# Expert outputs scattered into token order tile by tile, and loaded densely in the last stage

## The chip, the cores and the metric

The kernel runs on one core of a Trainium2 chip. A core has five engines that work side by side, each on its own instruction stream: PE (TensorE, matmuls and transposes), DVE (VectorE), ACT (ScalarE), POOL (GpSimd) and SP (SyncE, which mostly issues DMAs). They meet through semaphores. Sixteen DMA engines move data between device memory and the on-chip memory SBUF; matmul results land in PSUM. The metric is the device time of one launch in microseconds (us).

## What is computed

One layer of an audio tower over 16 x 256 tokens of width 256, in float32: a token projection with a GELU, attention with 16 heads, and a mixture of experts with two of eight experts per token plus a gated shared expert. The part that matters here:

```python
logits = xf @ router_w
probs = jax.nn.softmax(logits, axis=-1)
topw, topi = jax.lax.top_k(probs, 2)
combine = jnp.zeros((n, 8)).at[jnp.arange(n)[:, None], topi].add(topw)
h = silu(jnp.einsum('nd,edf->nef', xf, w1))
ye = jnp.einsum('nef,efd->ned', h, w2)
routed = jnp.einsum('ne,ned->nd', combine, ye)
gu = xf @ shared_gate_up
shared = silu(gu[:, :256]) * gu[:, 256:] @ shared_down
return routed + sigmoid(xf @ shared_gate_w) * shared
```

The residual stream is added, and token 0 of each of the 16 sequences is left out of the output, so a sequence gives 255 rows.

## The kernel before

Tokens are worked on in 8 groups of 512 (4 tiles of 128 rows). There are three blocks with a barrier at the end of each: `token_phase`, `attention_phase` and `expert_phase`. Float32 products are made of three passes over high and low parts (`three`, L65 to L67), so each operand is split into a `_hi` part (a copy) and a `_lo` part (a subtraction).

`attention_phase` is one software pipeline: 8 groups of 16 units, where the router of group g-1 runs between the units of group g. For each row the router finds two slots (`slot_now`) in a table `x_slots` in device memory in which every expert has its own region. In units 12 to 15 POOL scatters the normalised rows `z2` into it with 8 indirect DMAs (L1102), two per unit. The router of the last group has no attention beside it: it runs alone after group 7. `tables` on DVE then makes the list of row tiles per expert, and SP and ACT fill the rest of each expert's last tile (`fill_up`). POOL waits for its scatters, and the block's barrier follows (L343).

`expert_phase` starts with a loop over 72 tiles of 128 rows. SP loads tile n+6 into `xg` (L1227) and stores the result of tile n from `yg` into `y_slots` in slot order (L1232). PE transposes, multiplies by the expert's two matrices and transposes between them; ACT and DVE make the high and low parts; DVE copies the result to `yg` (L1494). PE sets the order. Experts 0 and 1 are loaded and split by ACT and DVE, experts 2 to 7 and the shared expert are loaded on POOL's queue (L1210, L1211) and split by POOL (L1600, L1604); six weight splits and a larger one of the shared expert.

The last stage goes over the 8 groups. PE computes the shared expert (`shared_hidden`, `transpose_z`, `shared_rows`); ACT, DVE take turns behind it. Once all tiles are stored, POOL fetches each token's two expert rows with `gather`: per tile a copy of two slot numbers to `place_now` (L1620) and two indirect DMAs (L1624) into `back`. DVE adds them, weighted (`add_back`, L1554), then the gated shared rows (`add_shared`, L1565). SP stores a group with two DMAs:

```python
sp.dma_start(out[bass.ds(2 * g, 2), 0:P - 1, :].rearrange("b p d -> p b d"),
             rows[1:P, :, 0, :]).then_inc(s_out, 16)          # L1237: 127 partitions
sp.dma_start(out[bass.ds(2 * g, 2), P - 1:N - 1, :].rearrange("b p d -> p b d"),
             rows[:, :, 1, :]).then_inc(s_out, 16)            # L1239: 128 partitions
```

`z`, the normalised input of the shared expert, is loaded by ACT two groups ahead, 512 KB at a time (L1458).

## Time and profile before

| | us |
|---|---|
| median of 3 runs (lowest, highest) | 1255.91 (1255.13, 1256.11) |
| span of the profiled execution | 1250.2 |
| busy: PE | 1076.8 (86%) |
| busy: DVE | 834.0 (67%) |
| busy: ACT | 676.0 (54%) |
| busy: POOL | 342.7 (27%) |
| DMA, all sixteen engines, moved | 64.31 MB |

The page gives no time of the profiled execution other than its span; the runs' median is 5.7 us longer, and that difference is start and end outside the span. Times in the rows are microseconds from the span's start. "Idle before" in brackets names what ended the wait. A POOL row DMA_INDIRECT is the time in which POOL makes the descriptors, not the transfer. SPq, ACTq and PEq rows are the sequencer's own: the time that a DMA's issue holds the queue. Indirect transfers stand in queue q0, SP's in q1, ACT's in q10.

### The profile page before, as it was taken

To read this page: it belongs to the slowest core of one execution; us is meant where nothing else is said; L and a number is where in the kernel's file an instruction comes from. 1 tells how busy PE (TensorE), PEld (TensorE's weight loads), DVE (VectorE), ACT (ScalarE), POOL (GpSimd) and SP (SyncE) were. 2 spreads that over 40 slices of the span, in tenths; PEclk is the share of its full clock that TensorE was granted. 3 is DMA by queue.
4 is the path that set the end of the run, shared out by engine and by line. 5 is a ranking of instruction groups with operands and counts; after the bars stand their busy time and mean duration, and the time that the engine had idled before them with its cause. 6 is when DMAs were issued, how large, how long until landed. Compare 5 with 4: busy or idle time off the path is not lost. (4 is left out here: it accounts for less than half of the span.)

```text
span 1250.2 us, 26008 instructions
## 1 busy us (share of the span) xinstructions
PE 1076.8 (86%) x8010; PEld 884.1 (71%) x8011; DVE 834.0 (67%) x2247; ACT 676.0 (54%) x2116; POOL 342.7 (27%) x405
## 2 busy tenths in 40 slices
PE   7989999999999999999999999999732999987770
PEld 6766787777767778677777877877622899976660
DVE  3757758876885885888578588588544555655661
ACT  4557647755773774776476477477412455532210
POOL 0021212242132124224213322411314800026660
PEclk9989999999999999999999999999965999998885
DMA  7100000000000000000000000000005544434531
GB/s 239 48 5 1 1 2 18 1 35 18 0 17 18 17 0 34 17 0 25 26 0 9 25 17 0 34 18 1 35 37 190 174 135 134 148 115 130 164 111 55
DMA packets 46177, 64.31 MB, mean 51 GB/s; under 512 B 6232, under 2 KB 38744, under 8 KB 46104
## 3 DMA queue, kind: packets, MB, share of 16 engines
q1 hardware_dynamic: 35832, 37.51, 9.2%
q0 software_dynamic: 7328, 20.72, 4.9%
q10 hardware_dynamic: 2944, 5.24, 1.3%
q8 instruction: 29, 0.48, 0.2%
q14 instruction: 44, 0.36, 0.1%
HBM read 36.07 MB, written 27.38 MB: 51 GB/s over the span
## 5 line engine op out<-in xcount | busy, mean ns | idle before, releaser
L702 ACT ACTIVATE prob<-s_ps,nmax 128x255 f32<-128x255 f32 x512 | 239.6, 481 | 275.1 <-DVE nmax L815 273.4
L1084 POOL TENSOR_SCALAR prob<-prob,rinv 128x255 f32<-128x255 f32 x128 | 126.2, 986 | 599.7 <-DVE rinv L834 599.7
L560 PE MATMUL o_ps<-probT,v 128*64 128x256 f32 x1024 | 140.4, 393 | 45.2 <-ACT probT L727 43.4
L815 DVE TENSOR_REDUCE nmax<-s_ps 128x2 f32<-128x510 f32 x256 | 165.0, 675 | 19.0 <-PE s_ps L532 9.4
L560 PEld LDWEIGHTS o_ps<-probT,v 128*64 128x64 f32 x1024 | 70.5, 137 | 108.0 <-ACT v L723 52.2
L547 PE MATMUL pT_ps<-ident,prob 128*128 128x128 f32 x1024 | 134.0, 274 | 0.1
L547 PEld LDWEIGHTS pT_ps<-ident,prob 128*128 128x128 f32 x1024 | 115.6, 141 | 2.5 <-DVE prob L837 1.5
L837 DVE TENSOR_SCALAR prob<-prob,rinv 128x255 f32<-128x255 f32 x256 | 106.9, 460 | 4.5
L702 ACT ACTIVATION_READ_ACCUMULATOR prob<-s_ps,nmax 128x1 f32 x512 | 109.0, 213 | 0.0
L843 DVE COPY probT<-pT_ps 128x512 f32<-128x512 f32 x128 | 87.0, 680 | 8.5 <-PE pT_ps L547 7.9
L532 PE MATMUL s_ps<-k_hi,q_lo 64*128 64x256 f32 x512 | 85.7, 331 | 0.7 <-DVE k_lo L822 0.7
L65 PE MATMUL v_ps<-wv_hi,zT_lo 128*128 128x256 f32 x256 | 85.2, 333 | 0.8 <-ACT v L723 0.8
L832 DVE TENSOR_SCALAR rsum_eps<-rsum 128x4 f32<-128x4 f32 x128 | 21.6, 169 | 92.7 <-ACT prob L702 91.0
L727 ACT ACTIVATE probT<-pT_ps 128x512 f32<-128x512 f32 x128 | 77.3, 604 | 0.8 <-PE pT_ps L547 0.8
L532 PEld LDWEIGHTS s_ps<-k_hi,q_lo 64*128 64x128 f32 x512 | 48.2, 185 | 39.5 <-issue 19.9
L1102 POOL DMA_INDIRECT expert_in_rows<-z,slot_now x64 | 64.2, 1004 | 36.2 <-DVE slot_now L916 20.4
L1624 POOL DMA_INDIRECT back<-expert_out_rows,place_now x64 | 63.8, 998 | 35.7 <-POOL place_now L1620 21.9
L65 PE MATMUL proj_ps<-wo_hi,oT_lo 128*128 128x256 f32 x256 | 73.2, 286 | 0.0
L67 PE MATMUL v_ps<-wv_hi,zT_hi 128*128 128x256 f32 x256 | 72.5, 283 | 0.0
L66 PE MATMUL v_ps<-wv_lo,zT_hi 128*128 128x256 f32 x256 | 72.4, 283 | 0.0
L532 PE MATMUL s_ps<-k_lo,q_hi 64*128 64x256 f32 x512 | 72.4, 279 | 0.0
L66 PE MATMUL proj_ps<-wo_lo,oT_hi 128*128 128x256 f32 x256 | 72.4, 283 | 0.0
(250 smaller groups left out, 2983.2 us busy)
## 6 DMA issues: line engine op xcount, KB each, us to landing
xg<-expert_in_rows SPq DMA_DIRECT2D x72, 128.0 KB, 2.0
expert_out_rows<-yg SPq DMA_DIRECT2D x72, 128.0 KB, 1.9
xin<-in_x_dram SPq DMA_DIRECT2D x8, 512.0 KB, 4.9
z_rows<-z SPq DMA_DIRECT2D x8, 512.0 KB, 2.6
z<-z_rows ACTq DMA_DIRECT2D x7, 512.0 KB
out_dram<-resid SPq DMA_DIRECT2D x8, 256.0 KB
out_dram<-resid SPq DMA_DIRECT2D x8, 254.0 KB
raw_up<-in_L_ffn_w_dram POOLq DMA_DIRECT2D x6, 256.0 KB, 4.6
```

The source lines that it names most:

```text
L65: pe.matmul(out, wl, xh, start=start, stop=False, skip_group_check=True)
L66: pe.matmul(out, wh, xl, start=False, stop=False, skip_group_check=True)
L67: return pe.matmul(out, wh, xh, start=False, stop=stop, skip_group_check=True)
L532: m = pe.matmul(s_ps[h][:, qt * N:(qt + 1) * N], a[part, rows], k[part, keys], start=n == 0, stop=n == 2)
L547: m = pe.transpose(pT_ps[h][:, o:o + P], prob[u_par(i)][:, h, qt, kt * P:(kt + 1) * P], ident[:])
L560: m = pe.matmul(o_ps[h * DH:(h + 1) * DH, 0:N], vt[:, 2 * b + kt, col:col + DH], probT[u_par(i)][:, h, kt, :], start=kt == 0, stop=kt == 1)
L702: m = act.activation(prob[u_par(i)][:, h, qt, 1:N], s_ps[h][:, qt * N + 1:(qt + 1) * N], ACT.Exp, bias=nmax[u_par(i)][:, n:n + 1], accum_o ...
L727: act.activation(probT[u_par(i)][:, 0, :, :], pT_ps[0][:].rearrange("p (k q) -> p k q", k=2), ACT.Copy).then_inc(s_pA, 1)
L815: dve.tensor_reduce(nmax[u_par(i)][:, 2 * h:2 * h + 2], s_ps[h][:].rearrange("p (q k) -> p q k", q=2)[:, :, 1:N], AX_X, ALU.max, negate=Tr ...
L837: m = dve.tensor_scalar(prob[k][:, 0, qt, 1:N], prob[k][:, 0, qt, 1:N], rinv[k][:, qt:qt + 1], None, ALU.mult)
L843: dve.tensor_copy(probT[u_par(i)][:, 1, :, :], pT_ps[1][:].rearrange("p (k q) -> p k q", k=2)).then_inc(s_pB, 1)
L1084: pool.tensor_scalar(prob[k][:, 1, 0, 1:N], prob[k][:, 1, 0, 1:N], rinv[k][:, 2:3], None, ALU.mult).then_inc(s_nB, 1)
```

## The change

Each row now carries where its result belongs. `x_slots` gets 8 more columns per row (`XW` = 264); before each scatter POOL writes the row's place in token order, 2 x token + choice, into column 256 of `z2`, and the second scatter of a tile waits for the first one to land, since the mark is overwritten. The spare rows get places behind the real ones, so that SP and ACT store two DMAs per padded region instead of one, and 8 spare tiles are stored at the start of attention. In the expert loop DVE copies the places from `xg` to `y_at`, and POOL scatters each finished tile straight into token order; SP only loads. The experts' weights from the third on are loaded on SP's queue, and POOL splits them between its scatters. The last stage loads 1 MB per group densely into one of two buffers, which lie where `raw_up` was. ACT scales the first choice's rows, POOL adds them and also makes the low part of the hidden activations, DVE adds the second choice's. Semaphores of the first two blocks are merged without a change in what waits for what.

```diff
+XW = D + 8
+SPARE = TILES - TOP * ROWS // P
@@ attention_phase, SP @@
+            for n in range(SPARE):
+                pad(sp, x_slots[E * CAP + n * P:E * CAP + (n + 1) * P, :], E + n)
...
-                sp.wait_ge(s_scat, 16 * GT * TOP * (r + 1))
+                for t in range(GT):
+                    sp.wait_ge(s_scat[t], 16 * TOP * r + 16 * TOP)
@@ attention_phase, POOL, units 12 to 15 @@
+                    for t in (2 * half, 2 * half + 1):
+                        if n > 0:
+                            pool.wait_ge(s_scat[t], 16 * TOP * r + 16)
+                        pool.sem_inc(s_pgo, 1)
+                        pool.tensor_scalar(z2[:, t, D:D + 1], dest[:, t:t + 1], float(n), None,
+                                           ALU.add).then_inc(s_marked, 1)
+                        pool.wait_ge(s_marked, TOP * GT * r + GT * n + t + 1)
+                        pool.sem_inc(s_pgo, 1)
                         pool.indirect_dma_start(
-                            x_slots, bass.IndirectOffsetOnAxis(ap=slot_now[:, n // TOP, n % TOP:n % TOP + 1], axis=0),
-                            z2[:, n // TOP, :], None).then_inc(s_scat, 16)
+                            x_slots, bass.IndirectOffsetOnAxis(ap=slot_now[:, t, n:n + 1], axis=0),
+                            z2[:, t, :], None).then_inc(s_scat[t], 16)
@@ expert_phase, SP @@
-                sp.dma_start(y_slots[bass.ds(P * n, P), :], yg[k % BUFS][:]).then_inc(s_st[k % BUFS], 16)
+            def load_back(g, k):
+                sp.dma_start(back[k].rearrange("p t k d -> p (t k d)"),
+                             y_rows[bass.ds(TOP * GR * g, TOP * GR), :].rearrange("(p s) d -> p (s d)", s=TOP * GT)
+                             ).then_inc(s_back[k], 16)
...
-            for k in range(BUFS):
-                sp.sem_inc(s_st[k], FREE_D)
             for k in range(BUFS):
                 load(0, k, True)
+            for e in range(BY_POOL, E):
+                load_expert(sp, e)
+            sp.dma_start(raw_gu[:], gate_up.rearrange("(c p) f -> p c f", p=P)).then_inc(s_raw_gu, 16)
...
-            with sp.Fori(0, GROUPS - 2) as g:
-                store_group(g)
+            for k in range(UNROLL):
+                sp.wait_ge(s_st[k], 16 * TURNS)
+            for k in range(2):
+                load_back(k, k)
+            with sp.Fori(0, GROUPS // 2 - 1) as h:
+                for k in range(2):
+                    sp.wait_ge(s_used, 2 * GT * h + GT * k + GT)
+                    load_back(2 * h + k + 2, k)
+                    store_group(2 * h + k)
@@ expert_phase, ACT, before the next group's SiLUs @@
+            def scale_first(g, k, at):
+                act.activation(share_first[:], shares[:, bass.ds(GT * g, GT), 0:1], ACT.Copy).then_inc(s_share1, 1)
+                act.wait_ge(s_back[k], at)
+                act.wait_ge(s_share1, g + 1)
+                for t in range(GT):
+                    act.activation(back[k][:, t, 0, :], back[k][:, t, 0, :], ACT.Copy,
+                                   scale=share_first[:, t, :]).then_inc(s_scaled, 1)
@@ expert_phase, DVE, in x_lo @@
+                if not isinstance(r, int) or r > 0:
+                    dve.wait_ge(s_st[k], 16 * r)
+                dve.tensor_copy(y_at[k][:], xg[k % BUFS][:, D:D + 1]).then_inc(s_at, 1)
@@ expert_phase, POOL @@
+                pool.wait_ge(s_at, n + 1)
+                pool.wait_ge(s_yc, n + 1)
                 pool.sem_inc(s_pgo, 1)
-                for k in range(TOP):
-                    pool.indirect_dma_start(back[:, t, k, :], None, y_slots,
-                                            bass.IndirectOffsetOnAxis(ap=place_now[:, t, k:k + 1], axis=0)
-                                            ).then_inc(s_back[t], 16)
+                pool.indirect_dma_start(y_rows, bass.IndirectOffsetOnAxis(ap=y_at[k][:, 0:1], axis=0), yg[k][:], None
+                                        ).then_inc(s_st[k], 16)
+            between = {(0, 5): 4, (0, 11): 5, (1, 5): 6, (1, 11): 7}
...
+            def add_first(g, k):
+                for t in range(GT):
+                    rows = resid[:, GT * g + t, :]
+                    pool.wait_ge(s_scaled, GT * g + t + 1)
+                    pool.tensor_tensor(rows, rows, back[k][:, t, 0, :], ALU.add).then_inc(s_first, 1)
```

The order in which the engines get their instructions shows three places. First POOL, the router of the last group up to the block's end; before:

```order
L1092 TENSOR_SCALAR var_eps<-mean_var 128x4 [waits row_mean_var]
L1094 TENSOR_TENSOR rstd<-var_eps,half_neg 128x4 [waits row_var_eps]
L1102 DMA expert_in_rows<-z,slot_now 33920x256 [waits slots_ready]
L1102 DMA expert_in_rows<-z,slot_now 33920x256 x7
L343 UNCONDITIONAL_BRANCH [waits rows_scattered]
```

and of the change:

```order
L1125 TENSOR_SCALAR dest<-dest 128x4
L1133 TENSOR_SCALAR z<-dest 128x1 [waits slots_ready,dest_ready]
L1137 DMA expert_in_rows<-z,slot_now 34816x264 [waits rows_marked]
L1133 TENSOR_SCALAR z<-dest 128x1
L1137 DMA expert_in_rows<-z,slot_now 34816x264 [waits rows_marked]
...
L1133 TENSOR_SCALAR z<-dest 128x1 [waits rows0_scattered]
L1137 DMA expert_in_rows<-z,slot_now 34816x264 [waits rows_marked]
...
L349 UNCONDITIONAL_BRANCH [waits rows2_scattered,rows3_scattered,rows1_scattered,rows0_scattered]
```

Eight scatters in a row have become eight pairs of a mark (`z<-dest`) and a scatter that waits for it. Next POOL in the expert block, from the weights on (`back` is fetched by gathers before; `up_space` is the memory of `raw_up`); before:

```order
L1600 CAST up_hi<-raw_up 128x2x256 [waits expert_split,expert2_in]
...
L1604 TENSOR_TENSOR sd_lo<-raw_sd,sd_hi 128x512
L1620 COPY place_now<-places 128x2 [waits all_yg_stored,places_ready]
L1624 DMA back<-expert_out_rows,place_now 128x256 [waits place_now_ready]
L1624 DMA back<-expert_out_rows,place_now 128x256
```

and of the change:

```order
L1633 TENSOR_TENSOR dn_lo<-raw_down,dn_hi 128x2x256
L1652 DMA expert_out_rows<-yg,y_at 10240x256 [waits y_at_ready,yg_ready] x6
L1629 CAST up_hi<-up_space 128x2x256 [waits expert4_in]
L1629 CAST dn_hi<-raw_down 128x2x256
L1633 TENSOR_TENSOR up_lo<-up_space,up_hi 128x2x256 [waits expert_hi_by_pool]
L1633 TENSOR_TENSOR dn_lo<-raw_down,dn_hi 128x2x256
L1652 DMA expert_out_rows<-yg,y_at 10240x256 [waits y_at_ready,yg_ready] x6
```

POOL, which had nothing between its last split and the end of the loop, now has 72 scatters there, six between two splits. Last SP in the last stage; before:

```order
L1260 UNCONDITIONAL_BRANCH [waits yg4_stored,yg3_stored,yg5_stored,yg2_stored,yg0_stored,yg1_stored]
...
L1237 ISA [waits rows_complete]
L1237 REGISTER_ALU
L1237 DMA out_dram<-resid 127x2x256
L1239 ISA
L1239 DMA out_dram<-resid 128x2x256
```

and of the change:

```order
L1267 ISA [waits back_used]
L1267 DMA up_space<-expert_out_rows 128x2048
L1272 ISA
L1274 ISA [waits rows_complete]
L1274 REGISTER_ALU
L1274 DMA out_dram<-resid 127x2x256
L1276 ISA
L1276 DMA out_dram<-resid 128x2x256
```

The load of the group after next stands on SP's queue ahead of each pair of stores.

## Rows read from the trace of the kernel before

**Rows 1.** Windows: busy us (instructions) per engine, PE clock, DMA share, GB/s.
```profile
core 0: us, PE busy (x) PEld busy (x) DVE busy (x) ACT busy (x) POOL busy (x), PEclk, DMA share, GB/s
1040.00:1060.00 20.00, 19.90 (x169) 19.54 (x168) 12.47 (x33) 10.93 (x33) 0.00 (x0) 1.00 0.42 127
...
1180.00:1200.00 20.00, 15.63 (x99) 13.75 (x97) 12.64 (x28) 6.38 (x11) 12.93 (x19) 1.00 0.44 135
...
1225.00:1230.00 5.00, 0.00 (x0) 0.00 (x0) 1.71 (x5) 0.00 (x0) 0.00 (x0) 0.50 0.07 24
```

**Rows 2.** Timeline of POOL, last stage: start, us, engine, line, instruction, [idle before].
```profile
1125.70 0.19 POOL L1620 COPY place_now<-places 128x2 uint32 x1
1126.70 0.98 POOL L1624 DMA_INDIRECT back<-expert_out_rows,place_now  x1 [0.81 <-POOL place_now L1620]
1127.98 0.97 POOL L1624 DMA_INDIRECT back<-expert_out_rows,place_now  x1 [0.30 <-issue]
```

**Rows 3.** Timeline of SP's queue, last stage: first store, longest hold, last hold.
```profile
1133.18 0.33 SPq L1237 DMA_DIRECT2D out_dram<-resid  x1
...
1177.15 14.53 SPq L1239 DMA_DIRECT2D out_dram<-resid  x1
...
1232.92 10.76 SPq L1239 DMA_DIRECT2D out_dram<-resid  x1
```

**Rows 4.** DMA view of 1225 to 1250.2 us, in 40 slices.
```profile
GB/s 24 24 24 23 24 24 24 24 24 24 24 23 244 195 24 24 24 24 24 23 24 24 24 24 24 23 24 24 24 24 189 247 28 23 24 24 24 24 20 0
```

**Rows 5.** DMA view of 1134.3 to 1250.2 us: packets, MB, share of 16 engines.
```profile
q0 software_dynamic: 2497, 6.82, 20.4%
q1 hardware_dynamic: 4214, 4.18, 10.7%
q10 hardware_dynamic: 576, 2.10, 5.3%
```

**Rows 6.** Timeline of POOL in a unit of the attention loop.
```profile
783.95 1.09 POOL L1102 DMA_INDIRECT expert_in_rows<-z,slot_now  x1 [0.18 <-issue]
...
786.33 0.74 POOL L1078 TENSOR_TENSOR resid<-resid,bo_row 128x256 f32 x1
788.33 0.99 POOL L1084 TENSOR_SCALAR prob<-prob,rinv 128x255 f32<-128x255 f32 x1 [1.26 <-DVE rinv L834]
```

**Rows 7.** Timeline at the hand-over: first and last of eight scatters, the next block.
```profile
934.73 1.09 POOL L1102 DMA_INDIRECT expert_in_rows<-z,slot_now  x1 [20.44 <-DVE slot_now L916]
...
943.79 0.97 POOL L1102 DMA_INDIRECT expert_in_rows<-z,slot_now  x1 [0.30 <-issue]
...
951.96 1.23 DVE L1507 TENSOR_SCALAR passed<-slots,skips 128x64 f32<-128x64 f32 x7 [8.48 <-PEq L343]
```

**Rows 8.** Chain of waits at SP's start in the expert block: start, us.
```profile
952.28 0.28 SPq L1226
```

**Rows 9.** First tiles: POOL's splits, DVE's split of expert 1, SP, PE, window.
```profile
969.22 0.66 POOL L1600 CAST up_hi<-raw_up 128x512 fp32r<-128x512 f32 x1
...
973.00 0.60 POOL L1600 CAST up_hi<-raw_up 128x512 fp32r<-128x512 f32 x1
...
963.46 0.68 DVE L1475 TENSOR_TENSOR dn_lo<-raw_down,dn_hi 128x512 fp32r<-128x512 f32 x1
...
969.26 0.34 SPq L1227 DMA_DIRECT2D xg<-expert_in_rows  x1
...
975.23 0.44 PE L1277 MATMUL xgT_ps<-ident,xg 128*128 128x128 f32 x2 [2.09 <-DMA xg<-expert_in_rows]
...
965.00:969.00 4.00, 3.86 (x32) 3.83 (x33) 1.94 (x5) 2.17 (x7) 4.00 (x7) 1.00 0.99 345
```

**Rows 10.** Timeline of ACT and DVE ahead of the first store.
```profile
1118.72 1.15 ACT L1451 ACTIVATE h_hi<-h_full 128x512 fp32r<-128x512 f32 x2
...
1125.94 1.09 ACT L1437 ACTIVATE z3T_hi<-xgT_ps 128x512 fp32r<-128x512 f32 x2 [1.20 <-PE xgT_ps L1338]
...
1131.23 1.66 DVE L1565 SCALAR_TENSOR_TENSOR resid<-y_ps,gate_now,resid 128x256 f32 x4 [0.32 <-issue]
```

**Rows 11.** Instructions on tile `back`: duration ns min/median/max, first and last start.
```profile
L1624 POOL DMA_INDIRECT back<-expert_out_rows,place_now x64: 952/980/1502, 1113.5 to 1218.8; - x64
```

More of the change, by code:

```diff
@@ L195, in _ @@
         def _(pe):
-            pe.wait_ge(s_ident, 1)
+            pe.wait_ge(s_const, IDENT_SET)
             pe.wait_ge(s_ro, 16)
@@ L1158, in sem @@
             return ctx.enter_context(nc.semaphore(name))
-        raw_up, raw_down = sb("raw_up", [P, DC, E, F]), sb("raw_down", [P, FC, E, D])
+        up_space = sb("up_space", [P, DC * E * F])
+        raw_up = up_space[:].rearrange("p (c e f) -> p c e f", c=DC, e=E)
+        back = [up_space[:, k * GT * TOP * D:(k + 1) * GT * TOP * D].rearrange("p (t k d) -> p t k d", t=GT, k=TOP)
+                for k in range(2)]
+        raw_down = sb("raw_down", [P, FC, E, D])
         raw_gu, raw_sd = sb("raw_gu", [P, DC, 2 * F]), sb("raw_sd", [P, FC, D])
@@ L1464, in _ @@
             group(0, True, True, True)
-            with act.Fori(1, GROUPS - 2) as g:
-                group(g, False, True, True)
+            with act.Fori(0, GROUPS // 2 - 2) as h:
+                for k in range(2):
+                    scale_first(2 * h + k, k, 16 * h + 16)
+                    group(2 * h + k + 1, False, True, True)
+            scale_first(GROUPS - 4, 0, 16 * (GROUPS // 2 - 1))
+            group(GROUPS - 3, False, True, True)
+            scale_first(GROUPS - 3, 1, 16 * (GROUPS // 2 - 1))
             group(GROUPS - 2, False, True, False)
+            scale_first(GROUPS - 2, 0, 16 * (GROUPS // 2))
             group(GROUPS - 1, False, False, False)
+            scale_first(GROUPS - 1, 1, 16 * (GROUPS // 2))
         @block.vector
@@ L1567, in add_shared, with group @@
                                                  op1=ALU.add).then_inc(s_all, 1)
-            def group(g, first, last):
+            def group(g, k, first, last):
                 product(g, 0)
-                if not first:
-                    add_back(g - 1, 1)
                 product(g, 1)
@@ L1628, in _, with split_shared @@
-            pool.wait_ge(s_places, 1)
-            pool.wait_ge(s_stored, 1)
-            for t in range(GT):
-                gather(0, t, True)
-            with pool.Fori(1, GROUPS) as g:
-                for t in range(GT):
-                    gather(g, t, False)
+                split(e - BY_POOL, [(raw_up[:, :, e, :], up_hi[:, :, e, :], up_lo[:, :, e, :]),
+                                    (raw_down[:, :, e, :], dn_hi[:, :, e, :], dn_lo[:, :, e, :])], s_w)
+            def split_shared():
+                pool.wait_ge(s_raw_gu, 32)
+                split(E - BY_POOL, [(raw_gu[:], gu_hi[:], gu_lo[:]), (raw_sd[:], sd_hi[:], sd_lo[:])], s_gu_w)
@@ new lines, in _, with shared_lo @@
+            for r in range(2):
+                for k in range(UNROLL):
+                    scatter(r, k)
+                    if (r, k) in between:
+                        split_expert(between[r, k])
+            split_shared()
+            with pool.Fori(2, TURNS) as r:
+                for k in range(UNROLL):
+                    scatter(r, k)
+            def shared_lo(g):
+                for c in range(FC):
+                    pool.wait_ge(s_hhi, FC * g + c + 1)
+                    pool.tensor_tensor(h_lo[:, c, :], h_full[:, c, :], f32(h_hi[:, c, :]), ALU.subtract).then_inc(s_hlo, 1)
@@ new lines, in add_first @@
+            def add_first(g, k):
+                for t in range(GT):
+                    rows = resid[:, GT * g + t, :]
+                    pool.wait_ge(s_scaled, GT * g + t + 1)
+                    pool.tensor_tensor(rows, rows, back[k][:, t, 0, :], ALU.add).then_inc(s_first, 1)
+            shared_lo(0)
+            with pool.Fori(0, GROUPS // 2 - 1) as h:
+                for k in range(2):
+                    add_first(2 * h + k, k)
+                    shared_lo(2 * h + k + 1)
+            add_first(GROUPS - 2, 0)
```

242 lines of the change are left out of this document (111 added, 131 removed).

## The prediction

> **What bounds the kernel now.** I read the page's busy shares first, then the windows stage by stage, then each engine's timeline at the places that the diff touches, then the DMA view of the end. PE (TensorE) is busy for most of the span, so the question is what the change does where PE is not the limit. There are three such places: the hand-over from attention to the experts (934 to 960 us), the first tiles of the expert loop (960 to 977), and the last stage, which adds the expert rows back and stores the result (from 1109).
>
> In the expert loop PE is busy 19.90 of 20 us [rows 1], and a tile leaves every 1.9 us. In the last stage it is not: 15.63 of 20 us, and nothing from 1225 on [rows 1]. Two candidates set the pace there. The one that the change aims at is POOL (GpSimd): copy 0.19, gap 0.81, gather 0.98, gap 0.30, gather 0.97, so 3.25 us for two gathers and 13.0 for a group of four tiles [rows 2]. The other is the output store. SP issues two DMAs for a group, L1237 with 127 partitions and L1239 with 128, and the second holds SP's queue for 10.8 to 14.5 us [rows 3]. The last 25 us say why: a flat 24 GB/s with two short bursts [rows 4], at a share of 0.07, which is one of sixteen engines [rows 1]. 254 KB at 24.2 GB/s is 10.75 us, and the last L1239 is held for 10.76 us [rows 3]. So the 127-partition store goes through one DMA engine, and what comes behind it on SP waits for that engine.
>
> Is this engine busy all the time? From 1134.3 us to the end the queues moved 6.82 MB (q0, gathers), 4.18 MB (q1, stores) and 2.10 MB (q10, z) [rows 5]. If gathers, z and L1239 are spread evenly and all of L1237 is on one engine, that engine carries 8 x 254 KB + 8 x 16 KB, 91.4 us at 24.2 GB/s, and (6.82 + 2.10) MB / 16 = 0.557 MB, 23.0 us more: 114.4 us. From its first store's data to its end the stage has about 115 us. **The engine that carries the 127-partition stores is full, and it ends the kernel**; POOL's gathers only run at nearly the same pace. The Trainium skill's page "DMA: Bandwidth & Descriptors", section "Why a DMA increments its semaphore by 16 and not by 1", states that 127 partitions put everything on one engine; by that rule the change, which leaves this store alone, cannot end before its eight stores have gone through one engine, and the trace agrees (24 GB/s at a share of 0.07).
>
> **The change part by part.**
>
> *Attention, steady state.* Each of the 64 scatters on POOL now waits for an instruction that marks its rows. An indirect DMA that waits for the copy ahead of it costs 0.19 + 0.81 + 0.98 us, one that follows another 0.30 + 0.97 [rows 2], so I price a marked scatter at 1.97 us against 1.27. In the loop a unit (two scatters, one 0.99 us normalisation, at one place 0.74 us of bias) lasts about 5.5 us [rows 6]; with the marks POOL needs 4.9 us, and at the one place 5.7. What it is late there PE hardly sees, since it first transposes the other head. The padding stores (32 small DMAs instead of 9) and z in 1 KB pieces go over idle queues. Cost 0; if the cover fails, about 0.3 us in each of seven groups, 2 us.
>
> *Hand-over to the experts.* After the last group nothing hides the eight scatters. Before, the first starts 0.83 us after the slots are ready, the last ends at 944.76, and the next block starts at 951.96, 7.2 us later, behind the barrier of line 343 [rows 7]. After, 8 x 1.97 = 15.8 us from 933.95 end at 949.75: **+5.0 us**, if the 7.2 us stay. Bounds: +1, if a mark overlaps with its scatter as at 783.95, where 0.18 us lie between an instruction and a scatter that has nothing to wait for [rows 6]; +6.5, if the second scatter of a tile has to wait for the first one's landing (it comes 7.9 us later). I take the upper half, since the waiting form of [rows 2] is the same pair of instructions. The padding stores on SP and ACT double, from 4 us to some 6, and still end by 942, ahead of POOL.
>
> *Start of the loop.* SP loses six semaphore increments ahead of its first tile load, which starts with the table read at 952.28 [rows 8] though the barrier is passed at 951.9: **-0.4 us**. The expert weights move from POOL's queue to SP's, between tile loads 5 and 6. SP would start them at 958.5, at 0.5 us each, end at 965.5, and then issue tile loads 6 and 7. 3.9 MB at 345 GB/s [rows 9] are done at 970, so tile 6 lands near 972, where PE wants it at 970.6: 1.5 us of waiting, against the 2.09 us that PE waited at 975.23 for tile 7, whose load left at 969.26 behind a store [rows 9]. **-0.6 us**, bounds -2 (no wait at all) and +2 (the load lands in 5.97 us, as the one at 969.26 did).
>
> *Loop.* 72 stores leave SP, 72 scatters go to POOL, DVE gets 72 copies of one column and is busy 12.47 of 20 us [rows 1], waiting for PE before each output copy, so these are free. POOL must carry seven splits and 72 scatters. A split is 3.78 us (969.22 to 973.00) [rows 9], the shared one half as much again: 28.3 us. A scatter whose rows are long ready needs 1.27 us; one that waits starts 0.83 us after its release [rows 7] and takes 0.97, 1.80 in all, just under the tile's 1.9. POOL starts when DVE has split expert 1, at 964.1 [rows 9]; the code places the later splits after scatters 5, 11, 17 and 23. Stepping through it, the shared split ends at about 1022, five tiles late with twelve buffers, and the last scatter ends at 1110.4. Cost 0. Split weights stay ahead of use: expert 4 at 983, first wanted at 1020.
>
> *Last stage.* Removed: 8 gathers and 4 copies per group on POOL. Added: one load of 1 MB on SP, four scalings on ACT, four adds of 0.74 us on POOL [rows 6]; the low parts move from DVE to POOL. With 1.5 groups in 20 us [rows 1], PE needs 10.4 us a group as before, DVE about 6 instead of 8.4, ACT 4.3 and at most 1.6 more, POOL 5.5. None comes near 14. What counts is when the store engine starts and what it carries. The last scatter is seen at about 1112, 1 MB lands by 1118 to 1120, and ACT scales it behind h_hi, which ends at 1119.87, with 2 us to spare ahead of its next SiLUs. z_hi of group 2 stays at 1125.94 [rows 10]; DVE's z_lo then ends at 1127.9, its share copy and four additions (1.66) at 1130.0, and SP's third load leaves there, ahead of the first store at 1132. Before, the first store left at 1133.18 [rows 3]. So the engine starts **3.2 us** earlier. It carries the stores (91.4 us), six loads (6 x 1.05 MB / 16) and four z loads (4 x 0.52 MB / 16), 0.524 MB, 21.7 us: 113.1 against 114.4, **-1.3 us**. Together **-4.5 us**; bounds -8 (dense packets go faster than gathered ones, and short pauses close) and 0 (the first load lands 5 us late).
>
> Sum: +5.0 - 0.4 - 0.6 - 4.5 = -0.5 us on the span of 1250.2, so 1249.7. The median of the runs is 5.7 us above that span, and I add this: **1255.4 us**.
>
> **The rivals.**
>
> *The change does what it says* (0.10). If the gathers do not ride on the full engine, POOL was the limit, and the pace falls to what a pair of stores needs alone, 0.6 + 10.8 = 11.4 us. The end is then 1132 + 7 x 11.4 + 17.9 (the last pair, issued at 1232.3) = 1229.7, and with the +4.0 ahead of it the time is 1239.4 us. For it: POOL's 13.0 us of a group leave it little idle. Against it: SP's hold of 14.53 us in the middle against 10.76 at the end [rows 3].
>
> *The scatters fall behind in the loop* (0.12; slower). If each scatter keeps its 0.81 us gap though its waits are met, POOL's pitch is 1.78 us, and 964.1 + 28.3 + 72 x 1.78 = 1120.6 instead of 1110.4: DVE stalls on the twelve buffers and the loop ends 10.2 us later, **1265.6 us**. It decides from a pitch of (1110.4 - 964.1 - 28.3) / 72 = 1.64 us. Against it: 0.18 us in [rows 6]. For it: 0.81 us after each copy, and single gathers of 1.50 us [rows 11].
>
> [...]
>
> *The hand-over isn't POOL's* (0.06). If the 7.2 us behind the last scatter belong to something that started earlier, the +5.0 falls away: 1250.4 us.
>
> **How the numbers follow.** The forecast has 0.72, with 1250 to 1260 as its own range from the bounds above. A measurement tells about 0.2%, 2.5 us. Of the 0.72, 0.21 lies more than that below the median of before, 0.37 within, 0.14 above. Faster: 0.21 + 0.10 + 0.06 = 0.37; same 0.37; slower 0.14 + 0.12 = 0.26. The range, 1248 to 1266, leaves out the first rival and the tails.
>
> **What the changed profile would show.** Eight scatters about 2.0 us apart behind the last group, and the expert block starting near 957. A wait of PE for tile 6 instead of 7. Scatters in the loop 1.27 us apart when late. The third load of 1 MB near 1134, the first store near 1136. SP's second store DMA held for 10 us and more, stores 13 to 15 us apart until the loads end, then 24 GB/s flat. I am wrong if stores are 11.4 us apart from the start, if the time from the last output copy to the end differs from 137 us by more than 5, or if DVE waits for scatters in the loop.

## The result, and the profile after

The changed kernel is slower. Its median is 1259.68 us (1259.46 to 1261.65, 4 runs), against 1255.52 us of the kernel before, run beside it (1253.72 to 1256.11, 4 runs). The ratio on record is 1.005, with a 95% interval of 1.0034 to 1.0065: 4 to 8 us lost. (The two medians alone give 1.0033. The kernel before was run again beside the experiments, with medians of 1253.2 to 1254.1 us, and against those it would be 1.0044 to 1.0052.) The forecast was 1255.4 us, that is no change; the measured time lies inside its range of 1248 to 1266.

| | before | after |
|---|---|---|
| profiled execution, time / span, us | 1252.0 / 1250.2 | 1261.65 / 1259.9 |
| busy PE, DVE, ACT, us | 1076.8, 834.0, 676.0 | 1076.6, 827.3, 688.9 |
| busy POOL, us | 342.7 | 398.6 |
| DMA moved, MB | 64.31 | 65.88 |

(Wherever the runs of these two kernels list both, an execution's time is its span plus 1.7 to 1.8 us, so the profiled one of before took about 1252.0 us.)

The useful way to compare is to cut both spans at three events that each trace shows: the start of the last cast to `slot_now` (attention and router done), and the first and the last copy to `yg` (expert loop begins and ends to deliver).

| us | last slots | slots to first yg | first to last yg | last yg to end | span |
|---|---|---|---|---|---|
| before | 933.7 | 33.6 | 140.8 | 142.0 | 1250.2 |
| after | 939.6 | 39.6 | 144.3 | 136.4 | 1259.9 |

Only the last stage gained. I go through the four pieces with the rows of after.

**Last stage.** Timeline of SP's queue in the changed kernel (start, us, engine, line, instruction): the stores of the first, second and last group.

```profile
1147.43 0.33 SPq L1274 DMA_DIRECT2D out_dram<-resid  x1
1147.98 9.37 SPq L1276 DMA_DIRECT2D out_dram<-resid  x1
...
1158.42 0.26 SPq L1274 DMA_DIRECT2D out_dram<-resid  x1
1158.90 14.22 SPq L1276 DMA_DIRECT2D out_dram<-resid  x1
...
1242.11 0.77 SPq L1274 DMA_DIRECT2D out_dram<-resid  x1
1242.93 10.26 SPq L1276 DMA_DIRECT2D out_dram<-resid  x1
```

They look as those of [rows 3] did: the store behind the 127-partition one holds SP for 9 to 14 us. Waits of the same kernel from 1150 to 1250 us (engine, line, waited for: us in total, times, longest), and the DMA view of 1220 to 1259.5 us in 40 slices:

```profile
ACT up_space L1500 <- DMA up_space<-expert_out_rows: 40.3, 5, 10.4
```
```profile
GB/s 389 57 33 25 21 24 25 24 24 25 30 267 25 24 24 24 25 24 24 25 24 24 171 135 24 25 24 24 24 25 24 24 24 25 270 27 25 24 24 15
```

The gathers are gone, and what ACT waits for now is the dense load (the buffer `back` lies in `up_space`, which names it here): its share on the full DMA engine queues behind the stores, median 8.1 us to land by the page. The flat 24 GB/s of [rows 4] is there again, now over the last 37 us or so, with short bursts in between.

**Hand-over.** Timeline of POOL behind the last slots (in brackets the idle time before, and what ended it):

```profile
940.07 0.23 POOL L1133 TENSOR_SCALAR z<-dest 128x1 f32<-128x1 f32 x1 [19.58 <-DVE slot_now L937]
941.13 1.10 POOL L1137 DMA_INDIRECT expert_in_rows<-z,slot_now  x1 [0.83 <-POOL z L1133]
942.27 0.23 POOL L1133 TENSOR_SCALAR z<-dest 128x1 f32<-128x1 f32 x1
943.32 1.06 POOL L1137 DMA_INDIRECT expert_in_rows<-z,slot_now  x1 [0.82 <-POOL z L1133]
...
956.19 1.06 POOL L1137 DMA_INDIRECT expert_in_rows<-z,slot_now  x1 [0.82 <-POOL z L1133]
```

Scatter starts are 2.15 us apart (941.13 to 956.19 in seven steps), where [rows 7] has 1.29. The last one ends at 957.25 and SP's first tile load leaves at 965.25, 8.0 us later (before: 944.76 and 953.03, 8.3 us). From the start of the last cast to the end of the last scatter it is 17.6 us instead of 11.0. The first output then follows the first tile load by 14.0 us, where it was 14.3.

**Start of the loop.** Timeline of SP and PE at the first tiles, and DVE's output copies:

```profile
971.21 0.44 SPq L1246 DMA_DIRECT2D up_space<-in_L_ffn_w_dram  x1
...
978.03 0.77 SPq L1284 DMA_DIRECT2D raw_sd<-n_L_ffn_shared_down_dram  x1
979.88 10.41 SPq L1264 DMA_DIRECT2D xg<-expert_in_rows  x7
```
```profile
987.06 0.69 PE L1319 MATMUL xgT_ps<-ident,xg 128*128 128x128 f32 x2 [3.98 <-DMA xg<-expert_in_rows]
```
```profile
982.89 0.42 DVE L1553 COPY yg<-y_ps 128x256 f32<-128x256 f32 x1 [0.38 <-PE y_ps L69]
990.35 0.42 DVE L1553 COPY yg<-y_ps 128x256 f32<-128x256 f32 x1 [1.66 <-PE y_ps L69]
993.56 0.42 DVE L1553 COPY yg<-y_ps 128x256 f32<-128x256 f32 x1 [1.46 <-PE y_ps L69]
995.38 0.42 DVE L1553 COPY yg<-y_ps 128x256 f32<-128x256 f32 x1 [0.37 <-PE y_ps L69]
```

Fourteen weight loads stand between tile loads 5 and 6. Tile load 6 leaves at 979.88 and lands near 987; PE waits 3.98 us, and the outputs show steps of 7.46 and 3.21 us where the others are 1.84: 7.0 us lost. Before, it was 2.7 us (4.18 and 2.22 against 1.87). The rest of the loop is 0.8 us shorter than before.

**The loop itself** is clean. POOL late behind its splits, then scattering (first row from 1050 us on):

```profile
1050.29 0.96 POOL L1652 DMA_INDIRECT expert_out_rows<-yg,y_at  x1 [0.30 <-issue]
1051.56 0.97 POOL L1652 DMA_INDIRECT expert_out_rows<-yg,y_at  x1 [0.30 <-issue]
```

1.27 us apart, as foreseen, and the only engines that DVE's waits between 1000 and 1120 us name are PE and ACT.

**Attention.** One unit on POOL, DVE and PE, the unit of [rows 6] in the changed kernel:

```profile
786.97 0.98 POOL L1111 TENSOR_SCALAR prob<-prob,rinv 128x255 f32<-128x255 f32 x1 [5.59 <-DVE rinv L855]
788.03 0.23 POOL L1125 TENSOR_SCALAR dest<-dest 128x4 f32<-128x4 f32 x1
788.45 0.23 POOL L1133 TENSOR_SCALAR z<-dest 128x1 f32<-128x1 f32 x1 [0.20 <-POOL dest L1125]
789.51 1.11 POOL L1137 DMA_INDIRECT expert_in_rows<-z,slot_now  x1 [0.83 <-POOL z L1133]
790.65 0.23 POOL L1133 TENSOR_SCALAR z<-dest 128x1 f32<-128x1 f32 x1
791.70 1.06 POOL L1137 DMA_INDIRECT expert_in_rows<-z,slot_now  x1 [0.82 <-POOL z L1133]
792.79 0.74 POOL L1105 TENSOR_TENSOR resid<-resid,bo_row 128x256 f32 x1
793.51 1.20 POOL L1111 TENSOR_SCALAR prob<-prob,rinv 128x255 f32<-128x255 f32 x1
```
```profile
792.12 0.18 DVE L855 RECIPROCAL rinv<-rsum_eps 128x4 f32<-128x4 f32 x1
792.33 1.58 DVE L858 TENSOR_SCALAR prob<-prob,rinv 128x255 f32<-128x255 f32 x2
```
```profile
794.77 0.66 PE L568 MATMUL pT_ps<-ident,prob 128*128 128x128 f32 x4 [0.15 <-POOL prob L1111]
```

Two things are to be seen. POOL has no time to spare: from one normalisation to the next it needs 6.54 us (786.97 to 793.51), where a unit lasts 5.5 [rows 6]. `rinv` is ready at 792.3, POOL takes it up at 793.51 (before, it had waited 1.26 us for it, [rows 6]) and PE then waits for POOL (0.15 us here). And DVE's scaling L858, two instructions, takes 1.58 us: the first 0.61 us, beside the end of a scatter, the second 1.04 us, beside POOL's addition. In the kernel before the same pair took 0.84 (0.35 and 0.57), with neither of the two beside it, only POOL's normalisation (timeline of DVE, before):

```profile
788.15 0.84 DVE L837 TENSOR_SCALAR prob<-prob,rinv 128x255 f32<-128x255 f32 x2
```

The page of after agrees over all groups. Its row of PE's transposes ends with 3.9 us idle, most of it by POOL's `prob`, where the page of before has 0.1:

```profile
L547 PE MATMUL pT_ps<-ident,prob 128*128 128x128 f32 x1024 | 134.0, 274 | 0.1
L568 PE MATMUL pT_ps<-ident,prob 128*128 128x128 f32 x1024 | 135.4, 274 | 3.9 <-POOL prob L1111 3.3
```

### The profile page after: what moved, and what is told of

The parts are those of the page before. It is cut to its first block and busy times, and to the rows that moved or that the text cites. A ratio compares the mean times of both kernels' runs of the same rounds, so it can differ in the third digit from the quotient of the medians.

```text
span 1259.9 us, 26246 instructions
## 1 busy us (share of the span) xinstructions
PE 1076.6 (85%) x8010; PEld 882.9 (70%) x8011; DVE 827.3 (66%) x2254; ACT 688.9 (55%) x2156; POOL 398.6 (32%) x493
## 2 busy tenths in 40 slices
DMA packets 46357, 65.88 MB, mean 52 GB/s; under 512 B 7752, under 2 KB 39368, under 8 KB 45256
## 5 line engine op out<-in xcount | busy, mean ns | idle before, releaser
L858 DVE TENSOR_SCALAR prob<-prob,rinv 128x255 f32<-128x255 f32 x256 | 112.8, 483 | 4.5
L1652 POOL DMA_INDIRECT expert_out_rows<-yg,y_at x72 | 69.9, 970 | 51.5 <-DVE yg L1553 35.0
L1137 POOL DMA_INDIRECT expert_in_rows<-z,slot_now x64 | 68.8, 1075 | 52.7 <-POOL z L1133 51.0
```

The lines of the kernel that those rows point to most:

```text
L858: m = dve.tensor_scalar(prob[k][:, 0, qt, 1:N], prob[k][:, 0, qt, 1:N], rinv[k][:, qt:qt + 1], None, ALU.mult)
```

## Experiments

Four questions were open: what ends the last stage, what delays the start of the loop, what the marks cost in attention and at the hand-over, and whether the gains add. Every kernel was run with its own runs of the kernel before beside it (medians 1253.16, 1254.10 and 1253.83 us in the three sets).

**What ends the last stage: the store is cut.** The same edit in the kernel before and in the changed one:

```diff
-                sp.dma_start(out[bass.ds(2 * g, 2), 0:P - 1, :].rearrange("b p d -> p b d"),
-                             rows[1:P, :, 0, :]).then_inc(s_out, 16)
+                sp.dma_start(out[bass.ds(2 * g, 2), 0:112, :].rearrange("b p d -> p b d"),
+                             rows[1:113, :, 0, :]).then_inc(s_out, 16)
+                sp.dma_start(out[bass.ds(2 * g, 2), 112:P - 1, :].rearrange("b p d -> p b d"),
+                             rows[113:P, :, 0, :]).then_inc(s_out, 16)
...
```

> The kernel before, with the 127-partition output store of each group cut in two, 112 and 15 partitions; nothing else. Theory (one DMA engine carries each 127-partition store and ends the kernel): SP's queue is no longer held for 10 us and more behind the store, the last stage goes to the pace of POOL's gathers, 13.0 us a group, and the end follows the last gather (it started at 1218.8 us before) by some 7 us instead of 31: 15 to 24 us less, about 1232 to 1240 us. Rival (POOL's gathers set the pace of the stage, the engine only runs along): 0 to 5 us less. Rival (128-partition stores are as slow, the hold is the destination's row pattern): no change, and holds of 10 us on the 112-partition store.

Measured: 1233.62 us, ratio 0.985 (0.983 to 0.9869), 19.5 us less. Last yg to end fell from 142.0 to 121.0 us. Timeline of SP in this kernel: no hold of 10 us any more.

```profile
1191.63 0.32 SPq L1237 DMA_DIRECT2D out_dram<-resid  x1
1192.19 0.34 SPq L1239 DMA_DIRECT2D out_dram<-resid  x1
1192.74 0.40 SPq L1241 DMA_DIRECT2D out_dram<-resid  x1
```

What is late next is what the forecast's rival had named, POOL and its gathers: DVE waits 31.6 us in total for them from 1120 to 1225 us, and stores are 11.3 to 14.2 us apart.

> The changed kernel with the same cut of the store. Theory (the last stage after is bound by nothing but that engine): the stage goes to PE's pace, 10.4 us a group, and from the last output copy to the end it takes 24 + 7 x 10.4 + 5 = 102 us instead of 136: about 1226 us, that is 32 to 36 us less than after, and some 10 us less than before with the same cut, since POOL's gathers are gone. Rival (the 1 MB loads, 8 us each, hold the additions back): 11 to 13 us a group, 1235 to 1245 us.

Measured: 1212.18 us, ratio 0.9678 (0.9658 to 0.9698), 47 us less than after, where 32 to 36 had been expected, and 21 us less than the kernel before with the same cut. The stage takes 87.3 us instead of 136.4; the theory had 102. Windows of this kernel (busy us and instructions of PE, PEld, DVE, ACT and POOL, then PE's clock, DMA share, GB/s):

```profile
1160.00:1180.00 20.00, 20.00 (x130) 17.93 (x129) 13.73 (x31) 11.35 (x24) 10.89 (x13) 1.00 0.69 229
```

against the changed kernel as it was:

```profile
1180.00:1200.00 20.00, 12.56 (x68) 10.61 (x66) 7.72 (x15) 7.42 (x18) 7.23 (x9) 0.83 0.33 110
```

PE is busy throughout, and a group takes about 9 us (stores at 1166.20 and 1175.13, at 1184.40 and 1193.34), not the 10.4 us that I had scaled from PE's busy time between waits. The 1 MB load lands in 5.1 us instead of 8.1. The cut frees the full engine and SP's held queue at once; what each of them costs in the changed kernel isn't separated here.

To see whether it is the number of partitions that matters, the cut was moved to 120 and 7, 120 not being a multiple of 16 (shown against the kernel with the cut at 112):

```diff
-                sp.dma_start(out[bass.ds(2 * g, 2), 0:112, :].rearrange("b p d -> p b d"),
-                             rows[1:113, :, 0, :]).then_inc(s_out, 16)
+                sp.dma_start(out[bass.ds(2 * g, 2), 0:120, :].rearrange("b p d -> p b d"),
+                             rows[1:121, :, 0, :]).then_inc(s_out, 16)
...
```

> The changed kernel with the 127-partition store cut in 120 and 7 partitions instead of 112 and 15. If a store spreads over all engines only where its partitions are a multiple of 16, and goes over a few where they are not, 120 partitions use 15, 8 or 1 engines: with 15 or 8 the stage keeps PE's pace and the span is that of the 112 cut, 1211 us; with one engine stores are again 10 us and more long (240 KB at 24 GB/s) and the span is 1250 us or more.

Measured: 1209.83 us in one run, the last stage 85.7 us. All instructions on the store's line, duration ns min/median/max:

```profile
L1274 SPq DMA_DIRECT2D out_dram<-resid x8: 338/352/423, 1144.7 to 1204.3; - x8
```

120 partitions are as good as 112, so a multiple of 16 isn't needed; 127 is the bad number here. Whether 120 goes over 15 or 8 engines can't be told from these times. The Trainium skill ("DMA: Bandwidth & Descriptors", "Why a DMA increments its semaphore by 16 and not by 1") gives the number of engines as the largest one up to 16 that divides the slowest dimension of both sides, here the partitions: 15 for 120 and 1 for 127. The runs agree for 127 (24 GB/s, the share of one engine), and for 120 they rule out 1.

**The start of the loop.** The fourteen weight loads go to POOL's queue, where they were before the change, behind the wait for tile 2:

```diff
@@ expert_phase, SP @@
-            for e in range(BY_POOL, E):
-                load_expert(sp, e)
...
@@ expert_phase, POOL @@
+            pool.wait_ge(s_x_in[2], 16)
+            for e in range(BY_POOL, E):
+                load_expert(pool, e)
...
```

> The changed kernel with the weights of experts 2 to 7 and of the shared expert loaded on POOL's queue again, ahead of the splits, instead of on SP's between tile loads 5 and 6. Theory (the 3.4 us lost at the start of the loop come from tile loads 6 and 7 standing behind the weights' issues on SP): PE's waits for tiles 6 and 7 shrink, first to last output copy takes 141 us instead of 144.3, 2 to 4 us less than after. Rival (the tiles wait for the bandwidth that the weights take, whoever issues them): no change within 1 us, PE's waits stay.

Measured: 1255.65 us, ratio 1.0026 (1.0012 to 1.004), 3 us less than after by the ratios. First to last yg is 137.1 us, 7 less than after and 4 less than before. Timeline of DVE: the outputs come 1.83 us apart from the first on, where every kernel with the weights on SP has the gap.

```profile
983.69 0.42 DVE L1549 COPY yg<-y_ps 128x256 f32<-128x256 f32 x1 [0.36 <-PE y_ps L69]
985.52 0.42 DVE L1549 COPY yg<-y_ps 128x256 f32<-128x256 f32 x1 [0.37 <-PE y_ps L69]
987.34 0.42 DVE L1549 COPY yg<-y_ps 128x256 f32<-128x256 f32 x1 [0.36 <-PE y_ps L69]
```

The weights still take their bandwidth (254 and 284 GB/s from 972 to 982 and to 992 us), so the rival falls: tile loads 6 and 7 leave at 972.88 and 974.23 instead of 979.88 and 981.24, the second of them lands 4.0 us later, and PE waits for neither. It also shows a gain that the change could have had. With the stores off SP's queue nothing delays tile load 7, and the 2.7 us that the kernel before lost there go too.

**The marks alone.** The kernel before with one more POOL instruction ahead of each scatter, which the scatter waits for. (Two semaphores of the router's weights are merged to make room, without a change in what waits for what.)

```diff
+                        pool.tensor_scalar(mark[:, n // TOP:n // TOP + 1], mark_in[:, n // TOP:n // TOP + 1], 1.0, None,
+                                           ALU.add).then_inc(s_marked, 1)
+                        pool.wait_ge(s_marked, TOP * GT * r + n + 1)
+                        pool.sem_inc(s_pgo, 1)
                         pool.indirect_dma_start(
...
```

> The kernel before, with one added POOL instruction per scatter in attention and the hand-over: it writes one column of a small tile (not of the rows), and the scatter waits for it. Rows, widths and stores are those of before. Theory (POOL's marks alone cost the attention and hand-over time of the changed kernel): the last slots come 3 to 5 us later than in the kernel before (933.7 and 935.8 us in its two profiles so far, 939.6 to 940.6 in three of the changed kernel), eight scatters at a pitch of 2.1 us make the hand-over 5 to 6 us longer, and the whole is 7 to 11 us slower than before. Rival (half of it comes from the wide rows and z's store in 1 KB pieces): only the hand-over, 5 to 6 us.

Measured: 1265.06 us, ratio 1.009 (1.007 to 1.0111), 11 us slower than before. The last slots come at 940.7, slots to first yg is 40.2 us. Marks alone reproduce both losses in full. In attention they do it in a somewhat different way: this kernel has no step of `dest`, so POOL's fullest unit is 6.1 us and not 6.5, and on its page PE's transposes wait for DVE's `prob` and not for POOL's:

```profile
L549 PE MATMUL pT_ps<-ident,prob 128*128 128x128 f32 x1024 | 134.5, 274 | 1.2 <-DVE prob L839 1.1
```

**The wide rows alone.** The kernel before with rows of 264 columns, z stored in 1 KB pieces, no marks:

```diff
-        z2 = sb("z2", [P, GT, D])
+        z2 = sb("z2", [P, GT, XW])
...
-                sp.dma_start(z_dram[bass.ds(r, 1)].rearrange("a p t d -> p (a t) d"), z2[:]).then_inc(s_zst, 16)
+                sp.dma_start(z_dram[bass.ds(r, 1)].rearrange("a p t d -> p (a t) d"), z2[:, :, 0:D]).then_inc(s_zst, 16)
...
```

> The kernel before with rows of 264 instead of 256 columns in z2, in the table of the experts' inputs and in the loaded tiles, so that z is stored in 1 KB pieces; no marks. Theory (marks only): within 1 us of before, the last slots at 934 to 936 us. Rival (wide rows cost something in attention, because the store or the scatters hold z2 longer): the last slots 2 to 4 us later, 2 to 4 us slower.

Measured: 1253.81 us, ratio 1.0 (0.999 to 1.0011), last slots at 934.2 us. The rival falls.

**Marks made early and in pairs.** In the changed kernel, with the same rows scattered:

```diff
                     if i == UNITS - GT:
                         pool.tensor_scalar(dest[:], dest[:], float(TOP * GR), None, ALU.add).then_inc(s_dest, 1)
+                        pool.wait_ge(s_z2, GT * r + GT)
...
+                        pool.tensor_scalar(z2[:, :, D:D + 1], dest[:].unsqueeze(2), 0.0, None,
+                                           ALU.add).then_inc(s_marked, 1)
                         pool.wait_ge(s_slot, r + 1)
...
+                    if n > 0:
+                        for t in (2 * half, 2 * half + 1):
+                            pool.wait_ge(s_scat[t], 16 * TOP * r + 16)
...
+                            pool.tensor_scalar(z2[:, t, D:D + 1], dest[:, t:t + 1], 1.0, None,
+                                               ALU.add).then_inc(s_marked, 1)
...
```

> The changed kernel with the marks of the first choice written by one instruction for all four tiles, before POOL waits for the slots, and those of the second choice in pairs ahead of two scatters, so that a scatter seldom waits for the instruction right ahead of it. Same rows scattered. Theory (both the 5.9 us of attention and the 6.0 us of the hand-over are POOL's marks: 0.23 us, a gap of 0.82 and a scatter of 1.06 behind it): eight scatters of the hand-over take 11 to 13 us instead of 17.5, so 4 to 6 us less there, and attention loses 1 to 3 of its 5.9: together 5 to 9 us less than after. Rival for attention (z stored in 1 KB pieces, or z2 free later): only the hand-over gains, 4 to 6 us, and the last slots stay at 939.6 us.

Measured: 1250.16 us, ratio 0.9981 (0.9969 to 0.9994): with this edit alone the kernel is 9 us faster than after, and a little faster than before. Slots to first yg is 36.3 us instead of 39.6, the last slots come at 937.2. Timeline of POOL at the hand-over, with the eight scatters between 938.31 and 950.07:

```profile
938.31 1.10 POOL L1146 DMA_INDIRECT expert_in_rows<-z,slot_now  x1 [18.54 <-DVE slot_now L937]
...
940.99 0.96 POOL L1146 DMA_INDIRECT expert_in_rows<-z,slot_now  x1 [0.30 <-issue]
942.25 0.96 POOL L1146 DMA_INDIRECT expert_in_rows<-z,slot_now  x1 [0.30 <-issue]
943.28 0.41 POOL L1140 TENSOR_SCALAR z<-dest 128x1 f32<-128x1 f32 x2
944.33 1.07 POOL L1146 DMA_INDIRECT expert_in_rows<-z,slot_now  x1 [0.63 <-POOL z L1140]
945.70 0.96 POOL L1146 DMA_INDIRECT expert_in_rows<-z,slot_now  x1 [0.30 <-DMA expert_in_rows<-z,slot_now]
...
949.11 0.96 POOL L1146 DMA_INDIRECT expert_in_rows<-z,slot_now  x1 [0.30 <-issue]
```

From the last cast to the end of the last scatter it is 12.9 us instead of 17.6, so the scatters gained the 4 to 6 us expected. The piece up to the first output shrank by 3.3 us only, because from the first tile load to that output it takes 15.5 us here and 14.0 in after. The edit doesn't touch that stretch, which lies between 13.9 and 16.2 us in the twelve profiles. In attention 2.4 us came back, and the timelines of POOL and DVE in that unit say what didn't: the displaced addition of POOL (790.65 to 791.39) now stands beside another DVE instruction, and that one was 0.17 us long before.

```profile
790.65 0.74 POOL L1105 TENSOR_TENSOR resid<-resid,bo_row 128x256 f32 x1
790.67 0.75 DVE L853 TENSOR_SCALAR rsum_eps<-rsum 128x4 f32<-128x4 f32 x1 [1.56 <-ACT prob L723]
```

**The bias additions one unit earlier.** This tests that reading: in the changed kernel, marks as they were,

```diff
-                    if 9 <= i < 9 + GT and not last:
-                        add_bias(g + 1, i - 9)
+                    if 8 <= i < 8 + GT and not last:
+                        add_bias(g + 1, i - 8)
```

> The changed kernel with POOL's four additions of the attention bias in units 8 to 11 instead of 9 to 12, so that the unit in which POOL marks and scatters for the first time carries none of them. Theory (the attention loss of the marks is made in this one unit: POOL ends 1.0 us late there, and the displaced addition of 0.74 us stands beside DVE's scaling of the probabilities, which takes 1.58 us instead of 0.84): six groups lose 0.2 to 0.3 us instead of 1.0, the last slots come at 935 to 937 us instead of 940, and the whole is 3 to 5 us faster than the changed kernel. Rival (every unit with marks costs its share): less than 1.5 us.

Measured: 1256.50 us, ratio 1.0015 (1.0003 to 1.0027), 4.4 us less than after by the ratios. The last slots come at 937.8 us. That is later than the theory's 937, because the router's last, lone interval grew from 51.6 to 53.0 us, for which I have no cause; the six intervals of the groups before it are 3.5 us shorter together. On the page DVE's L858 fell from a mean of 483 to 466 ns (before: 460), and PE's transposes waited 1.3 us for POOL's `prob` instead of 3.3. Part of what is left can be the marks' too: once in each group DVE's `rsum_eps` still takes 0.37 us instead of 0.17, beside a scatter.

**All together.** Store cut, weights on POOL's queue, early marks; and the same with the bias moved.

> The changed kernel with all three edits: output store cut in 112 and 15, weights on POOL's queue, marks early and in pairs. If the three losses are independent, their gains add: 45 us (store) + 8 (marks) + 4 (weights) below the changed kernel, so 1198 to 1204 us, about 50 us below before. Rival (the loop's gain is given back in the last stage, where scatters or splits then come late): 1204 to 1212 us.

> The kernel with the cut store, the weights on POOL's queue and the early, paired marks, and with the bias additions in units 8 to 11 as well. In e4 and e8 the addition of unit 12 stands beside DVE's smallest instruction of the softmax (0.75 instead of 0.17 us), and the last slots come at 937.2 to 937.5 us against 933.7 to 935.8 in kernels without marks. Theory: this 2 to 3 us comes back, last slots at 934 to 936, 1196 to 1198 us in all. Rival (what remains has another cause): as e8, 1199.5 us.

Measured: 1199.54 us, ratio 0.9562 (0.9545 to 0.958), and 1196.05 us, ratio 0.9545 (0.9522 to 0.9568): the gains add, and the second is 58 us below the kernel before. Its last slots come at 933.2 us, as without marks.

| us | last slots | slots to first yg | first to last yg | last yg to end | median |
|---|---|---|---|---|---|
| before, store cut | 935.8 | 35.0 | 141.5 | 121.0 | 1233.62 |
| before, marks only | 940.7 | 40.2 | 140.9 | 141.5 | 1265.06 |
| before, wide rows | 934.2 | 35.9 | 139.9 | 142.2 | 1253.81 |
| after, store cut | 940.6 | 39.6 | 143.9 | 87.3 | 1212.18 |
| after, cut at 120 | 940.6 | 39.9 | 141.9 | 85.7 | 1209.83 |
| after, weights on POOL | 940.2 | 39.8 | 137.1 | 136.5 | 1255.65 |
| after, early marks | 937.2 | 36.3 | 141.7 | 134.6 | 1250.16 |
| after, bias early | 937.8 | 39.8 | 142.6 | 134.8 | 1256.50 |
| three edits | 937.5 | 35.3 | 136.9 | 86.8 | 1199.54 |
| four edits | 933.2 | 35.9 | 136.8 | 86.8 | 1196.05 |

The columns also tell how far one profile can be trusted. Where nothing in a piece differs, it still varies by 2 to 2.6 us. The means of the profiles that share a piece with before and with after are: last slots 934.6 (3 profiles) and 940.4 (5, the marks-only kernel among them), slots to first yg 34.8 (3) and 39.8 (6, likewise), the loop 140.8 (4) and 142.9 (5), the end 141.9 (3) and 135.6 (4). The differences, +5.8, +5.0, +2.1 and -6.3 us, sum to +6.6, and the ratio of 1.005 means +6.3.

## Why the prediction was wrong

**Right: what bounds the last stage, and that the change doesn't touch it.** The engine that carries the 127-partition store ended both kernels; cutting the store alone took 19.5 us off the one and 47 off the other. The last stage was put at -4.5 us with bounds -8 and 0, and measured -6.3. Its two terms came out the other way round: the first store leaves 24.0 us after the last output copy instead of 25.0, so 1.0 us earlier where I had 3.2, and from the first store to the end it is 112.4 instead of 117.0 us, 4.6 us less where I had 1.3. No run shows why the second gained more.

**Right in kind, too small in size: the hand-over.** The pair of [rows 2], a copy and a scatter that waits for it, was the right form, but 1.97 us was foreseen and 2.15 seen. From the last cast to the end of the last scatter it is 17.6 us instead of 11.0: +6.6 where I had +5.0, as much as my upper bound, and not by that bound's mechanism, since no scatter waited for a landing. From there to the first tile load it is 0.3 us less (I had -0.4). That the piece up to the first output grew by just 5.0 as a mean over the profiles (6.0 between the first two) is luck: from the first tile load to the first output it took 1.2 us less on average in the kernels with marks (14.2 against 15.4, with single profiles from 13.9 to 16.2), for which I had no term and have no cause.

**Wrong: "attention, steady state: cost 0".** It costs 5.8 us, and this is the step that made the forecast fail. I had summed 5.7 us of work on POOL in the unit with the bias addition, against 5.5 of the unit. I wrote that PE hardly sees what POOL is late, and gave 0.3 us a group as the price of the failed cover. Seen was about 0.8 us in each of seven groups. The work in that unit is 6.54 us rather than 5.7: the step of `dest` and the gap behind it (0.42 us) were left out, two marked scatters take 4.34 us and not 3.94, and 0.08 us lie behind the normalisation. So POOL is 1.0 us late and not 0.2. And the displaced addition, with the scatter ahead of it, cost DVE 0.74 us in a pair on the softmax's path. Moving only that addition gave back 2.6 us of the time to the last slots (940.4 to 937.8) in spite of a longer last interval, early marks alone gave 3.0 (the mean of 937.2 and 937.5), and both together all of it. So the marks are the cause, and the full unit is where about half of the loss was made. How much of it came by POOL's lateness and how much by the DVE instructions beside its work stays open: the marks-only kernel lost as much with POOL only 0.6 us late and PE waiting for DVE's `prob`.

**Wrong: "start of the loop, -0.4 and -0.6".** The -0.4 came nearly (8.3 to 8.0 us, above); in place of the -0.6 the loop took 2.1 us more. The order of events was right (PE's wait moves to tile 6, whose load stands behind the weights), the size was not: SP needed 14.6 us from its first tile load to tile load 6 where I had 13.2, and the load landed some 7 us after its issue, where I had let it come in at the tail of the weights. At the place itself the outputs lost 7.0 us instead of 2.7, and as a mean over the profiles 5.8 instead of 2.8: +3.0, beyond the bound of +2 that I gave for a slow landing. The rest of the loop was 0.9 us shorter on average and took it back to +2.1.

**Right: the loop.** Late scatters run at 1.27 us, so the rival that put them at 1.78 us is refuted; DVE never waited for POOL. **Right against "the change does what it says":** stores are 11.0 to 16.0 us apart (1147.4, 1158.4, 1174.5 and so on), 13.5 on average against 14.2 before. The last two groups, behind the last load, are 11.6 us apart, which is the 11.4 that I had put for a pair of stores alone, and the first two 11.0. What I didn't price is the cut of the store: with it the changed kernel reaches 1212 us. **The rival "the hand-over isn't POOL's"** is refuted by the marks-only kernel.

**Half wrong: the 5.7 us outside the span.** An execution of this kernel takes 1.7 to 1.8 us more than its span. The rest was scatter: executions of before lay between 1249 and 1259 us, and the profiled one, about 1252.0, was among the faster. Adding the 5.7 us led to the right base all the same, since the forecast has to stand on the median; but they were no start and end.

With attention at +5.8 and the loop's start at +2.1 in place of 0 and -1.0, the same sum gives -0.5 + 5.8 + 3.1 = +8.4 us, or +6.6 with the measured last stage. In it the +5.0 stands for the whole piece from the last slots to the first output, which its terms only happen to match, and single profiles vary by 2 us a piece, so the tenths mean little.

## What to carry to other kernels

Find the resource that is full before weighing a rewrite beside it: here the rewrite was worth 21 us, but only once a store of 127 partitions had been cut in two, and without that cut it lost 6. When work is added to an engine "with slack", do the sum for its fullest unit, and look at what its displaced instructions will then stand beside on the engine that shares its ports. And when stores leave a queue, keep bulk loads out of the room that they free, if short loads that an engine waits for come next in it.

## What the runs showed of the hardware

- A DVE instruction of 0.17 us (128x4) took 0.75 us when POOL's 0.74 us addition had started 0.02 us before it, and a pair of 0.84 us took 1.58 us beside a scatter and the addition. A scatter does it too: in the marks-only kernel the same 0.17 us instruction took 0.47 us, from 793.22 to 793.68, beside a scatter that ended at 793.63. The Trainium skill ("SBUF — State Buffer", "SBUF: two separate sides") says that VectorE and GpSimd share a port pair which is locked for a whole instruction, so that the later one fully waits, where VectorE's instruction is in a two-port mode or has two SBUF inputs. This trace agrees for the addition, since DVE's instruction ended at 791.42, 0.03 us behind it (791.39); whether that instruction was in such a mode no trace says. Beside POOL's normalisation it doesn't look so: in the kernel before a DVE scaling that started at 788.42, 0.09 us behind it, ended at 788.99, and the normalisation at 789.32 (spans on POOL are rough).
- An indirect DMA of POOL starts 0.82 us after the instruction ahead if it waits for it, 0.18 us behind an instruction it doesn't wait for, and 0.30 us behind another indirect DMA. With a second mark between, 0.63 us pass after that one, which is again 0.82 us from the end of the mark it waits for (943.51 to 944.33 in the kernel with early marks). A scatter behind anything but another scatter mostly takes 1.02 to 1.11 us instead of 0.96.
- One 127-partition store of 254 KB on one DMA engine at 24 GB/s slowed a 1 MB load from 5.1 to 8.1 us to land. PE's granted clock was 1.00 (2.4 GHz) from 1160 to 1180 us in the kernel with the store cut, where it was busy for 20.00 of 20 us, and 0.83 on average, between the levels of 1.2 and 2.4 GHz, from 1180 to 1200 us in the changed one, where it was busy for 12.56.
